# One product of a two-layer graph network as three one-pass matmuls instead of one fp32 matmul, with the work around it in another order

## The chip, the cores and the metric

The kernel runs on one core of a Trainium2 chip. The metric is device time in microseconds (us), the median of several executions. Engines: PE is TensorE (matmul), DVE is VectorE, ACT is ScalarE, POOL is GpSimd, SP is SyncE, which here only issues DMAs.

## The reference

For each of 8 graphs (C = 1024 nodes, D = 256 features, DH = 512 hidden), with H = (adj != 0), w the first row of adj, Dn = 1/(H w) and Be = 1/(column sums of H):

```
m  = Be * (H^T x)                      # S1
z  = H m                               # S2, kept transposed
h  = relu(Dn * (z W1^T) + b1)          # P
h  = layer_norm(h) * gamma + beta
q  = h W2^T                            # Q, gamma folded into W2, beta into a row
m2 = Be * (H^T q)                      # S3
x1 = layer_norm(x + Dn * (H m2) + b2 + x)      # S4
v  = x1 WL^T                           # V, both halves of WL
o  = relu(v_left + (adj v_right) / deg)        # L
out = layer_norm(x1 + o)
```

Input, output and weights are float32, x is [8, 1024, 256] and adj [8, 1024, 1024].

## The kernel before

The nodes lie in NT = 8 tiles of 128. Each engine has its instruction stream written out by hand, one body per graph, and the streams meet in semaphores; an engine takes its instructions strictly in the order written. PE runs the stages S1, S2, P/Q, S3, S4, V, L and then S1 of the next graph. A product that must be exact in fp32 is a plain F32 matmul; S1 to S4 have one factor of zeros and ones (H), so the other factor is split into a high and a low part of type F32R (a rounded fp32), and each part is one F32R matmul.

The stretch around the change is the loop over steps s, on PE as on DVE and ACT. S2 makes z^T in four PSUM banks: its first half (nodes 0 to 511) runs before the loop, eight k-steps of four matmuls with 512 columns; its second half is dealt out over the first four loop steps (`SECOND_CHUNK`, k-steps 3, 2, 2, 1). ACT copies z^T to `zT` (L480). Step s then holds on PE: P(s), two F32 matmuls of 512 columns (L893); from s = 3 the four transposes TH(s-3) of the hidden rows (L901); from s = 4 Q(s-4), four F32 matmuls of 256 columns (L909). On DVE: hrow = P(s) * rDn + b1 (L675), the inverse root and the centring of tile s-1 (L574, L579), `moments` of tile s (L583, L585), q_f32 = Q(s-4) + a row (L689). On ACT: relu (L487), xnT out of the transposes (L494), the square root for the variance (L440), x_hi, the high part of q (L501). POOL makes the low part (L388, semaphore `q_split`).

S3, S4 and L go through `tiled` (L777): a first pass over k with two output tiles at once (`GROUP`), each k waiting for its input (`ready`), then the remaining tiles one by one. In S3, ACT and DVE make m_hi (L435) and m_lo (L590) from each finished tile; `sum_Dn` of the next graph (L558) is queued on DVE behind m_lo of tiles 3 to 7, and waits for the load of `raw`, which SP issues once Q(7) is done:

```
sp.wait_ge(*full("Q", NT - 1, b))
load_graph(b + 1)
...
for e in range(NT):
    take_m_lo("S3", e, b, NT + e)
    if more and e >= DN_LAG:
        sum_Dn(e - DN_LAG, b + 1, (raw_loaded[(e - DN_LAG) // 2], (b + 1) * IN_B))
```

Before the first graph a prologue transposes adj on PE while S1 of graph 0 runs as rows of adj arrive: per row tile c, transposes, S1 for six output tiles, and one weight's transposes (`BETWEEN`). `sum_bW2` (L621) runs on DVE in c = 6, in front of the building of H for c = 7 (L543). `PRODUCT_BANKS` says which PSUM bank each output takes.

Of the kernel before, what the change touches and what calls it, by code (L numbers as in the profile page):

```python
# [5 lines left out]
F32 = mybir.dt.float32  # L6
# [21 lines left out]
}  # L28
TRANSPOSE_BANKS = (6, 7)
N_BANKS = 8  # L30
GROUP = 2
SECOND_CHUNK = {0: (0, 1, 2), 1: (3, 4), 2: (5, 6), 3: (7,)}
LAG_T = 3
LAG_Q = 4
H_SLOTS = 4
# [3 lines left out]
def graph_net(nc, x, adj, W1, b1, gamma, beta, W2, b2, WL, out):  # L39
# [21 lines left out]
    BETWEEN = {1: ("gamma",), 3: ("W1", "W1"), 5: ("WL", "WL"), 6: ("W2", "W2")}  # L61
# [3 lines left out]
    def add_set(name, part):  # L65
        n = len(set_of)
        set_of[name, part] = TRANSPOSE_BANKS[n % 2], n // 2
# [9 lines left out]
    setup_fills = [0] * N_SIDE + [(len(set_of) + 1) // 2, len(set_of) // 2]  # L77
# [22 lines left out]
    for s in range(NT + LAG_Q):  # L100
        if s < NT:
            add_job("P", s)
        if 0 <= s - LAG_T < NT:
            add_job("TH", s - LAG_T)
        if 0 <= s - LAG_Q < NT:
            add_job("Q", s - LAG_Q)
# [12 lines left out]
    with ctx:  # L119
# [21 lines left out]
        xres, _, _ = place("xres", [P, NT, D], F32)  # L141
        w_row, _, _ = place("w_row", [P, C], F32)
        W1T, _, _ = place("W1T", [P, ND, DH], F32)
# [5 lines left out]
        x1T, _, _ = place("x1T", [P, 2, ND, P], F32)  # L149
        q_f32, q_at, _ = place("q_f32", [P, 2, D], F32)  # L150
        o_f32, _, _ = place("o_f32", [P, 2, D], F32)
        ident, _, _ = place("ident", [P, P], F32)
        small, _, _ = place("small", [P, 20, NT], F32)

        zT, _, nxt = place("zT", [P, ND, C], F32, raw_at)
        hrow, _, nxt = place("hrow", [P, H_SLOTS, DH], F32, nxt)
        xnT, _, _ = place("xnT", [P, 2, NH, P], F32, nxt)
# [4 lines left out]
        yv, _, _ = place("yv", [P, NT, YP], F32, HT_at)  # L162

        unread, _, _ = place("unread", [P, C], F32, q_at)
# [6 lines left out]
        gamma_n, _, _ = place("gamma_n", [P, P], F32, nxt)  # L171

        def col(n):
# [3 lines left out]
         std_o, rstd_o, gb) = (col(n) for n in range(16))  # L177
        gamma_c, bW2_c, eps_c = gb[:, 0:NH], gb[:, NH:NH + ND], small[:, 16, 0:1]
        stats, _, _ = place("stats", [P, 3, NT, 6], F32)
# [27 lines left out]
        relu_done = sem("relu_done")  # L207
        deg_done, rdeg_done, o_done, sum_done = (sem(n) for n in ("deg_done", "rdeg_done", "o_done", "sum_done"))
# [60 lines left out]
        def _(sp):  # L269
# [44 lines left out]
            load_first_rows(6)  # L314
            load_first_rows(7)
# [39 lines left out]
        def _(pool):  # L355
# [13 lines left out]

            for j in range(NT // 2):  # L370
                pool.wait_ge(first_x_loaded[j], 16)
            pool.wait_ge(bias_loaded, 16 * 2)
            pool.wait_ge(rDn_ready, 1)
# [26 lines left out]
        def _(act):  # L400
# [61 lines left out]
            for c in range(NT):  # L462
                take_adjT(c, 0)
                if c in BETWEEN:
                    take_set(BETWEEN[c][0], 0)
                if c % 2 == 0 and c + 2 < NT:
                    split_first_x_hi(c // 2 + 1)
                take_adjT(c, 1)
                if len(BETWEEN.get(c, ())) > 1:
                    take_set(BETWEEN[c][1], 1)  # L470
            for e in range(NT):
                take_m_hi("S1", e, 0, e)

            def graph(b, more):
                def take_zT(ch):
                    for d in range(ND):
                        act.wait_ge(*full("S2", ch * ND + d, b))
                        act.wait_ge(HT_ready, b * NT + NT)
                        act.wait_ge(dn_ready, b * NT + NT)
                        empties_bank(nc.scalar.activation(zT[:, d, ch * CH:(ch + 1) * CH],  # L480
                                                          bank("S2", ch * ND + d)[:, :], ACT.Copy), "S2", ch * ND + d)

                take_zT(0)
                for s in range(NT + LAG_Q):
                    if s < NT:
                        act.wait_ge(*emptied("P", s, b))
                        nc.scalar.activation(hrow[:, s % H_SLOTS, :], hrow[:, s % H_SLOTS, :], ACT.Relu)\  # L487
                          .then_inc(relu_done, 1)
                    if s == max(SECOND_CHUNK) - 1:
                        take_zT(1)  # L490
                    if 0 <= s - LAG_T < NT:
                        i = s - LAG_T
                        act.wait_ge(*full("TH", i, b))
                        empties_bank(nc.scalar.activation(xnT[:, i % 2, :, :].rearrange("p k c -> p (k c)"),  # L494
                                                          bank("TH", i)[:, :], ACT.Copy), "TH", i)
                    if s < NT:
                        root("h", 0, std_h, s, b)
                    if s >= LAG_Q:
                        i = s - LAG_Q
                        act.wait_ge(*emptied("Q", i, b))  # L500
                        nc.scalar.activation(x_hi[:, i, 0:D], q_f32[:, i % 2, :], ACT.Copy).then_inc(q_hi_done, 1)  # L501
# [38 lines left out]
        def _(dve):  # L540
# [10 lines left out]
            def sum_Dn(c, b, loaded):  # L551
# [6 lines left out]
                nc.vector.scalar_tensor_tensor(out=unread[:, :], in0=raw[:, c, :], scalar=0.0, in1=w_row[:, :],  # L558
# [3 lines left out]
            def build_rDn(b):  # L562
# [4 lines left out]
                dve.wait_ge(rDn_part, b * 3 + 2)  # L567
                nc.vector.reciprocal(dn_inv, dn_safe).then_inc(rDn_part, 1)
                dve.wait_ge(rDn_part, b * 3 + 3)
                nc.vector.tensor_tensor(rDn, dn_inv, dn_pos, ALU.mult).then_inc(rDn_ready, 1)  # L570
# [11 lines left out]
            def moments(norm, which, src, i, b):  # L582
                nc.vector.bn_stats(stats[:, which, i, :], src)  # L583
                dve.drain()
                nc.vector.bn_aggr(mv[:, which, i, :], stats[:, which, i, :]).then_inc(var_done[norm], 1)  # L585
# [56 lines left out]
            for c in range(NT):  # L642
# [14 lines left out]
            for e in range(NT):  # L657
# [3 lines left out]
                if e == 0:  # L661
                    dve.wait_ge(*set_full("bW2", 0))
                    nc.vector.tensor_copy(bW2_row[:, :], set_bank("bW2", 0)[:, 0:D])\
                      .then_inc(bank_empty[set_of["bW2", 0][0]], 1)
                if N_SIDE - 3 <= e < N_SIDE:
                    sum_Dn(e + NT - N_SIDE, 0, (first_rows_loaded[e + NT - N_SIDE], 16))
            build_rDn(0)

            def graph(b, more):
                dve.wait_ge(bias_loaded, 16 * 2)  # L670
                dve.wait_ge(rDn_ready, b + 1)
                for s in range(NT + LAG_Q):
                    if s < NT:
                        dve.wait_ge(*full("P", s, b))
                        empties_bank(nc.vector.scalar_tensor_tensor(  # L675
                            out=hrow[:, s % H_SLOTS, :], in0=bank("P", s)[:, :], scalar=rDn[:, s:s + 1],
                            in1=b1_row[:, :], op0=ALU.mult, op1=ALU.add), "P", s)
                    if 0 <= s - 1 < NT:
                        inverse_root("h", std_h, rstd_h, s - 1, b)
                        centre("h", 0, hrow[:, (s - 1) % H_SLOTS, :], rstd_h, s - 1, b)  # L680
                    if s < NT:
                        dve.wait_ge(relu_done, b * NT + s + 1)
                        moments("h", 0, hrow[:, s % H_SLOTS, :], s, b)
                    if s >= LAG_Q:
                        i = s - LAG_Q
                        dve.wait_ge(*full("Q", i, b))
                        if i >= 2:
                            dve.wait_ge(q_split, b * NT + i - 1)
                        empties_bank(nc.vector.tensor_tensor(q_f32[:, i % 2, :], bank("Q", i)[:, 0:D],  # L689
                                                             bW2_row[:, :], ALU.add), "Q", i)  # L690
                if more:
                    dve.wait_ge(q_split, b * NT + NT)
                for e in range(NT):
                    take_m_lo("S3", e, b, NT + e)
                    if more and e >= DN_LAG:
                        sum_Dn(e - DN_LAG, b + 1, (raw_loaded[(e - DN_LAG) // 2], (b + 1) * IN_B))

                dve.wait_ge(xb_ready, b * NT + NT)
                for i in range(NT + 1):
# [14 lines left out]
                    if i < NT:  # L714
                        if i == 0:
                            dve.drain()
                        nc.vector.bn_aggr(mv[:, 1, i, :], stats[:, 1, i, :]).then_inc(var_done["1"], 1)

                nc.vector.memset(yv[:, :, 2 * D:YP], 1.0).then_inc(y_ones, 1)
                if more:  # L720
                    for c in range(NT):
                        build_H_tile(c, b + 1)
                        if c >= NT - DN_LAG:
                            sum_Dn(c, b + 1, (raw_loaded[c // 2], (b + 1) * IN_B))
# [39 lines left out]
        def _(pe):  # L764
# [12 lines left out]
            def tiled(stage, b, n_cols, ready, parts, operands, before_last=None):  # L777
# [10 lines left out]
                for k in range(NT):  # L788
                    ready(k)
                    for i in range(GROUP):  # L790
# [3 lines left out]
                for i in range(GROUP, NT):  # L794
# [46 lines left out]
            for c in range(NT):  # L841
                pe.wait_ge(first_rows_loaded[c], 16)
                transpose_adj(c, 0)
                pe.wait_ge(H_ready, c + 1)
                pe.wait_ge(x_split, c + 1)
                for e in range(N_SIDE):
# [4 lines left out]
                    if e == 3:  # L851
# [4 lines left out]
            transpose_set("bW2", 0)  # L856
# [118 lines left out]
```

## Time and profile before

| | us |
|---|---|
| runs, not profiled: median, lowest, highest of 3 | 1104.91, 1104.28, 1105.42 |
| the profiled execution's own time | 1105.18 |
| its span, first to last instruction | 1103.6 |
| PE busy | 1090.7 (99%) |
| DVE busy | 699.1 (63%) |
| ACT busy | 317.0 (29%) |
| POOL busy | 182.6 (17%) |

The span lies 1.58 us below the execution's own time. Matmuls overlap each other at their ends, so a busy PE is not yet one at full pace; the pace of a matmul is read from the distance between its neighbours. The granted TensorE clock was 0.999 of full over the run.

### The profile page before, as it was taken

The page shows a single profiled execution, that of the slowest core. Times are in us where ns is not written, and L with a number is a line of the kernel's source. Part 1 is how long each engine was busy: PE and PEld are TensorE (multiplying, and loading weights), DVE is VectorE, ACT ScalarE, POOL GpSimd, SP SyncE. Part 2 cuts the span into 40 slices and gives each one's busy share as a digit, 9 for nine tenths or more (in the row PEclk, how much of TensorE's full clock was granted, in tenths as well). Part 3 has the DMA queues.
Part 4 walks back from the last instruction along what each step waited for, and adds up shares of the span by engine and source line. Part 5 has one row for each costly group of instructions (what it writes and reads, how often), then busy time and mean ns, then how long its engine had stood idle before and what let it go on. Part 6 is the DMA issues. An engine that isn't in the chain of part 4 may idle for free.

```text
span 1103.6 us, 18550 instructions
## 1 busy us (share of the span) xinstructions
PE 1090.7 (99%) x6107; PEld 895.7 (81%) x6107; DVE 699.1 (63%) x1845; ACT 317.0 (29%) x710; POOL 182.6 (17%) x256
## 2 busy tenths in 40 slices
PE   7999999999999999999999999999999999999997
PEld 7779697796978979688796978969788696887966
DVE  5666595576854768548685486755776746856326
ACT  5342212422133321333113331233301433024230
POOL 0312013210122102111040120401104020041000
PEclk9999999999999999999999999999999999999999
DMA  8117611167212471134611445116433075300001
GB/s 291 39 21 153 153 59 38 25 127 152 57 38 51 102 160 48 38 80 102 132 48 38 105 106 112 48 28 134 105 84 74 2 152 115 66 10 1 1 1 39
DMA packets 63871, 86.44 MB, mean 78 GB/s; under 512 B 8164, under 2 KB 53864, under 8 KB 63848
## 3 DMA queue, kind: packets, MB, share of 16 engines
q1 hardware_dynamic: 63376, 85.75, 33.9%
q10 hardware_dynamic: 472, 0.40, 0.1%
q8 instruction: 13, 0.21, 0.1%
q14 instruction: 10, 0.08, 0.0%
HBM read 77.73 MB, written 8.39 MB: 78 GB/s over the span
## 4 chain that ended last, share of the span: by engine, by line
PE 93%; DVE 4%; DMA 1%; SPq 1%; ACT 1%; issue 0%; DVEq 0%; ACTq 0%
PE bank L783 40%; PE bank L871 10%; PE bank L909 10%; PE bank L931 10%; PE bank L893 10%; PE bank L811 9%; PE bank L901 3%; PE bank L917 1%; DMA raw<-in_adj_dram 1%; DVE adjT L603 1%; DVE HT L608 1%; DVE o_f L740 0%; DVE xres L744 0%; ACT m_hi L435 0%; DVE stats L583 0%
## 5 line engine op out<-in xcount | busy, mean ns | idle before, releaser
L783 PE MATMUL bank<-yv,adjT 128*128 128x257 f32 x1024 | 223.3, 379 | 0.0
L783 PEld LDWEIGHTS bank<-yv,adjT 128*128 128x128 f32 x1024 | 193.6, 189 | 31.8 <-issue 3.8
L440 ACT ACTIVATE small<-mv,small 128x1 f32<-128x1 f32 x192 | 56.6, 295 | 361.9 <-DVE mv L585 266.4
L811 PE MATMUL bank<-x_hi,H 128*128 128x258 f32 x512 | 124.6, 290 | 1.2 <-issue 0.6
L783 PE MATMUL bank<-x_hi,H 128*128 128x256 f32 x512 | 122.6, 283 | 0.0
L783 PE MATMUL bank<-m_hi,HT 128*128 128x256 f32 x512 | 121.5, 280 | 0.0
L783 PE MATMUL bank<-x_lo,H 128*128 128x256 f32 x512 | 121.1, 280 | 0.0
L783 PE MATMUL bank<-m_lo,HT 128*128 128x256 f32 x512 | 120.8, 279 | 0.0
L811 PE MATMUL bank<-x_lo,H 128*128 128x256 f32 x512 | 119.6, 282 | 0.9 <-DVE H L543 0.9
L893 PE MATMUL bank<-W1T,zT 128*128 128x512 f32 x256 | 120.3, 592 | 0.0
L590 DVE SCALAR_TENSOR_TENSOR m_lo<-bank,small,m_hi 128x256 fp32r<-128x256 f32 x128 | 61.0, 483 | 92.8 <-ACT m_hi L435 92.8
L909 PE MATMUL bank<-gW2T,xnT 128*128 128x256 f32 x512 | 119.8, 379 | 0.0
L931 PE MATMUL bank<-WLT,x1T 128*128 128x512 f32 x256 | 119.1, 593 | 0.0
L378 POOL TENSOR_TENSOR xres<-x_in 128x256 f32<-128x256 f32 x64 | 43.6, 716 | 451.9 <-DMA out_dram<-xres 411.5
L435 ACT ACTIVATE m_hi<-bank,small 128x256 fp32r<-128x256 f32 x128 | 59.9, 475 | 182.7 <-DVE small L635 94.8
L871 PE MATMUL bank<-HT,m_hi 128*128 128x512 f32 x256 | 110.4, 431 | 0.2 <-DVE m_lo L590 0.2
L675 DVE SCALAR_TENSOR_TENSOR hrow<-bank,small,b_row 128x512 f32<-128x512 f32 x64 | 47.8, 747 | 96.0 <-PE bank L893 96.0
L871 PE MATMUL bank<-HT,m_lo 128*128 128x512 f32 x256 | 101.7, 397 | 0.0
L909 PEld LDWEIGHTS bank<-gW2T,xnT 128*128 128x128 f32 x512 | 92.9, 190 | 10.3
L783 PEld LDWEIGHTS bank<-x_hi,H 128*128 128x128 f32 x512 | 96.8, 189 | 0.2
L783 PEld LDWEIGHTS bank<-x_lo,H 128*128 128x128 f32 x512 | 96.2, 188 | 0.2
L783 PEld LDWEIGHTS bank<-m_lo,HT 128*128 128x128 f32 x512 | 96.1, 188 | 0.0
(84 smaller groups left out, 1620.6 us busy)
## 6 DMA issues: line engine op xcount, KB each, us to landing
raw<-in_adj_dram SPq DMA_DIRECT2D x112, 256.0 KB, 8.6
adjB<-in_adj_dram SPq DMA_DIRECT2D x224, 128.0 KB, 3.4
x_in<-in_x_dram SPq DMA_DIRECT2D x31, 256.0 KB, 4.7
out_dram<-xres SPq DMA_DIRECT2D x108, 64.0 KB, 1.6
raw<-in_adj_dram SPq DMA_DIRECT2D x8, 512.0 KB, 10.3
w_row<-in_adj_dram SPq DMA_DIRECT2D x8, 512.0 KB, 3.6
out_dram<-xres SPq DMA_DIRECT2D x4, 256.0 KB, 2.2
W1n<-in_L_gnn_W_dram SPq DMA_DIRECT2D x1, 512.0 KB, 10.8
```

The source lines that it names most:

```text
L378: nc.gpsimd.tensor_tensor(xres[:, t, :], x_in[:, t, :], x_in[:, t, :], ALU.add).then_inc(xb_part, 1)
L435: nc.scalar.activation(m_hi[:, e, :], bank(stage, e)[:, 0:D], ACT.Identity, scale=rBe[:, e:e + 1])\
L440: nc.scalar.activation(std[:, i:i + 1], mv[:, which, i, 1:2], ACT.Sqrt, bias=eps_c)\
L590: empties_bank(nc.vector.scalar_tensor_tensor(out=m_lo[:, e, :], in0=bank(stage, e)[:, 0:D], scalar=rBe[:, e:e + 1], in1=m_hi[:, e, :].bit ...
L675: empties_bank(nc.vector.scalar_tensor_tensor(out=hrow[:, s % H_SLOTS, :], in0=bank("P", s)[:, :], scalar=rDn[:, s:s + 1], in1=b1_row[:, : ...
L783: last = mm(bank(stage, i)[:, 0:n_cols], lhsT, rhs, start=(k == 0 and part == 0), stop=(k == NT - 1 and part == parts - 1))
L811: last = mm(*args, start=(c == 0 and n == 0), stop=(c == NT - 1 and n == 1))
L871: last = mm(bank("S2", job)[:, :], m[:, k, d * P:(d + 1) * P], HT[:, k, ch * CH:(ch + 1) * CH], start=(k == 0 and n == 0), stop=(k == NT - ...
L893: last = mm(bank("P", s)[:, :], zT[:, d, s * P:(s + 1) * P], W1T[:, d, :], start=(d == 0), stop=(d == ND - 1))
L901: last = nc.tensor.transpose(bank("TH", i)[:, k * P:(k + 1) * P], hrow[:, i % H_SLOTS, k * P:(k + 1) * P], ident[:, :])
L909: last = mm(bank("Q", i)[:, 0:D], xnT[:, i % 2, k, :], gW2T[:, k, :], start=(k == 0), stop=(k == NH - 1))
L931: last = mm(bank("V", i)[:, :], x1T[:, i % 2, d, :], WLT[:, d, :], start=(d == 0), stop=(d == ND - 1))
```

## The change

P = z W1^T is no longer an F32 matmul. z and W1 are each split: high = F32R(value * ROUND_DOWN), low = value - high. W1_low is scaled by 4096 (SPLIT), W1_cross = W1_high - scaled W1_low, and z_cross = z_high * (1 + 1/4096) - z. P is put together from three F32R products, z_cross W1_cross in a PSUM bank of its own (stage "M"), and z_high W1_high + z_low W1_low in another. Per tile DVE adds the two with their scales: M first, hrow = M * rDn_cross + b1, and then hrow = P * rDn_main + hrow. Of z, ACT makes the high part (in place of the copy), DVE the low and the cross part, both read from PSUM. The centring of h goes from DVE to ACT (`centre_h`, with a shift that DVE computes). S2's second half is spread over steps 0 to 2 (k-steps 4, 2, 2). TH lags P by 2 and Q by 3 steps instead of 3 and 4; Q comes ahead of TH; S3's first pass takes four tiles and has Q(5) to Q(7) and TH(6), TH(7) between its first k-steps. The layout of banks and SBUF follows. In the prologue, rows 6 and 7 of adj are loaded ahead of W2 and beta, W2's transposes and `sum_bW2` move from c = 6 to c = 7, both transposes of row tile 0 come ahead of its H, bW2's transposes move into S1(6), and the splitting of W1 is added on ACT and POOL.

```diff
-SECOND_CHUNK = {0: (0, 1, 2), 1: (3, 4), 2: (5, 6), 3: (7,)}
-LAG_T = 3
-LAG_Q = 4
-H_SLOTS = 4
+SECOND_CHUNK = {0: (0, 1, 2, 3), 1: (4, 5), 2: (6, 7)}
+LAG_T = 2
+LAG_Q = 3
+H_SLOTS = 3
...
             load_first_rows(5)
             sp.dma_start(WLn[:, :, :], WL.rearrange("(t p) d -> p t d", p=P)).then_inc(WL_loaded, 16)
+            load_first_rows(6)
+            load_first_rows(7)
             sp.dma_start(W2n[:, :, :], W2.rearrange("(t p) d -> p t d", p=P)).then_inc(W2_loaded, 16)
...
# ACT
+                act.wait_ge(HT_ready, b * NT + NT)
+                act.wait_ge(dn_ready, b * NT + NT)
+                take_z_high(0, 0)
+                take_z_high(0, 1)
                 for s in range(NT + LAG_Q):
+                    if s == max(SECOND_CHUNK):
+                        take_z_high(1, 0)
+                    if 0 <= s - 1 < NT:
+                        root("h", 0, std_h, s - 1, b)
+                    if s == max(SECOND_CHUNK):
+                        take_z_high(1, 1)
+                    if s == 1:
+                        centre_h(0)
+                    if 0 <= s - LAG_T < NT:
+                        act.wait_ge(*full("TH", s - LAG_T, b))
+                        empties_bank(nc.scalar.activation(xnT[:, :, :].rearrange("p k c -> p (k c)"),
+                                                          bank("TH", s - LAG_T)[:, :], ACT.Copy), "TH", s - LAG_T)
                     if s < NT:
                         act.wait_ge(*emptied("P", s, b))
                         nc.scalar.activation(hrow[:, s % H_SLOTS, :], hrow[:, s % H_SLOTS, :], ACT.Relu)\
                           .then_inc(relu_done, 1)
+                    if 1 <= s - 1 < NT:
+                        centre_h(s - 1)
+                    if s > LAG_Q:
+                        take_x_hi(s - LAG_Q - 1)
+                take_x_hi(NT - 1)
...
# DVE
+                take_z_low(0, 0)
+                take_z_low(0, 1)
                 for s in range(NT + LAG_Q):
+                    if s in (1, 2):
+                        moments_h(s - 1)
+                    if s < NT:
+                        dve.wait_ge(*full("M", s, b))
+                        empties_bank(nc.vector.scalar_tensor_tensor(
+                            out=hrow[:, s % H_SLOTS, :], in0=bank("M", s)[:, :], scalar=rDn_cross[:, s:s + 1],
+                            in1=b1_row[:, :], op0=ALU.mult, op1=ALU.add), "M", s)
+                    if 2 < s <= NT:
+                        moments_h(s - 1)
+                    if s == 1:
+                        shift_of(0)
+                    if s == max(SECOND_CHUNK):
+                        take_z_low(1, 0)
                     if s < NT:
                         dve.wait_ge(*full("P", s, b))
+                        dve.wait_ge(*emptied("M", s, b))
                         empties_bank(nc.vector.scalar_tensor_tensor(
-                            out=hrow[:, s % H_SLOTS, :], in0=bank("P", s)[:, :], scalar=rDn[:, s:s + 1],
-                            in1=b1_row[:, :], op0=ALU.mult, op1=ALU.add), "P", s)
+                            out=hrow[:, s % H_SLOTS, :], in0=bank("P", s)[:, :], scalar=rDn_main[:, s:s + 1],
+                            in1=hrow[:, s % H_SLOTS, :], op0=ALU.mult, op1=ALU.add), "P", s)
+                    if 1 < s <= NT:
+                        shift_of(s - 1)
+                    if s == max(SECOND_CHUNK):
+                        take_z_low(1, 1)
+                    if s > LAG_Q:
+                        take_q(s - LAG_Q - 1)
+                take_q(NT - 1)
...
# PE
+                        for d in range(ND):
+                            last = mm(bank("M", s)[:, :], z_cross[:, d, nodes], W1_cross[:, d, :],
                                       start=(d == 0), stop=(d == ND - 1))
+                        fills_bank(last, "M", s)
+                        pe.wait_ge(*free("P", s, b))
+                        for d in range(ND):
+                            mm(bank("P", s)[:, :], z_high[:, d, nodes], W1_high[:, d, :], start=(d == 0), stop=False)
+                            last = mm(bank("P", s)[:, :], z_low[:, d, nodes], W1_low[:, d, :],
+                                      start=False, stop=(d == ND - 1))
                         fills_bank(last, "P", s)
+                    if s >= LAG_Q:
+                        take_product_Q(s - LAG_Q)
+                    if s >= LAG_T:
+                        transpose_hidden(s - LAG_T)
...
                 tiled("S3", b, D, lambda c: pe.wait_ge(q_split, b * NT + c + 1), 2,
-                      lambda c, e, part: (H_columns(c, e), (x_hi, x_lo)[part][:, c, 0:D]))
+                      lambda c, e, part: (H_columns(c, e), (x_hi, x_lo)[part][:, c, 0:D]),
+                      group=4, behind_k=last_of_Q)
```

`take_z_low(ch, d)` is one subtraction (z_low, PSUM minus SBUF) and one scalar_tensor_tensor (z_cross, SBUF and PSUM), 512 columns each; `moments_h` is L583 and L585; `shift_of` is the reciprocal L574 and a 128x1 tensor_scalar; `take_q` is L689; `last_of_Q(c)` is Q(5+c) and TH(6+c), as far as there are any.

## Rows read from the trace of the kernel before

**Rows 1.** The page's first part: busy time and share of the span.

```profile
PE 1090.7 (99%) x6107; PEld 895.7 (81%) x6107; DVE 699.1 (63%) x1845; ACT 317.0 (29%) x710; POOL 182.6 (17%) x256
```

**Rows 2.** The critical chain in one graph: start us, us, what.

```profile
439.99 10.27 PE bank L871 x44
...
451.97 1.86 PE bank L871 x8
...
469.97 1.72 PE bank L893 x4
471.69 0.44 PE bank L901 x4
472.13 1.73 PE bank L909 x8
...
485.96 28.28 PE bank L783 x240
```

**Rows 3.** Groups of instructions by line and form, whole span.

```profile
L590 DVE SCALAR_TENSOR_TENSOR m_lo<-bank,small,m_hi 128x256 fp32r<-128x256 f32 x128 | 61.0, 483 | 92.8 <-ACT m_hi L435 92.8
L435 ACT ACTIVATE m_hi<-bank,small 128x256 fp32r<-128x256 f32 x128 | 59.9, 475 | 182.7 <-DVE small L635 94.8 <-PE bank L783 87.9
L675 DVE SCALAR_TENSOR_TENSOR hrow<-bank,small,b_row 128x512 f32<-128x512 f32 x64 | 47.8, 747 | 96.0 <-PE bank L893 96.0
L740 DVE SCALAR_TENSOR_TENSOR o_f<-bank,small,yv 128x256 f32<-128x256 f32 x64 | 30.6, 478 | 0.3
L689 DVE TENSOR_TENSOR q_f<-bank,bW_row 128x256 f32<-128x256 f32 x64 | 26.9, 420 | 44.9 <-PE bank L909 44.9
```

**Rows 4.** Timeline of VectorE in one loop step: start us, us, what [idle before].

```profile
471.73 0.75 DVE L675 SCALAR_TENSOR_TENSOR hrow<-bank,small,b_row 128x512 f32<-128x512 f32 x1 [1.12 <-PE bank L893]
472.39 0.15 DVE L574 RECIPROCAL small<-small 128x1 f32<-128x1 f32 x1
472.59 0.55 DVE L579 TENSOR_SCALAR hrow<-hrow,mv,small 128x512 f32<-128x512 f32 x1
473.18 0.69 DVE L583 BATCH_NORM_STATS2 stats<-hrow 128x6 f32<-128x512 f32 x1
473.95 0.18 DVE L585 BATCH_NORM_AGGREGATE mv<-stats 128x2 f32<-128x6 f32 x1
474.13 0.43 DVE L689 TENSOR_TENSOR q_f<-bank,bW_row 128x256 f32<-128x256 f32 x1
```

**Rows 5.** Timeline of ScalarE in the same graph's loop.

```profile
447.15 1.09 ACT L480 ACTIVATE zT<-bank 128x512 f32<-128x512 f32 x2 [1.85 <-PE bank L871]
...
476.40 0.63 ACT L487 ACTIVATE hrow<-hrow 128x512 f32<-128x512 f32 x1 [1.39 <-DVE hrow L675]
476.93 0.58 ACT L494 ACTIVATE xnT<-bank 128x512 f32<-128x512 f32 x1
478.04 0.29 ACT L440 ACTIVATE small<-mv,small 128x1 f32<-128x1 f32 x1 [0.53 <-DVE mv L585]
478.38 0.42 ACT L501 ACTIVATE x_hi<-q_f 128x256 fp32r<-128x256 f32 x1
478.71 0.58 ACT L494 ACTIVATE xnT<-bank 128x512 f32<-128x512 f32 x1
```

**Rows 6.** Timeline of SyncE in the same graph: issue of the load of raw.

```profile
485.99 7.82 SPq L273 DMA_DIRECT2D raw<-in_adj_dram  x16
```

**Rows 7.** Timeline of VectorE in S3 of the same graph: `sum_Dn` of tiles 2 and 4.

```profile
498.23 1.22 DVE L558 SCALAR_TENSOR_TENSOR unread<-raw,w_row 128x1024 f32<-128x1024 f32 x1
...
502.46 1.23 DVE L558 SCALAR_TENSOR_TENSOR unread<-raw,w_row 128x1024 f32<-128x1024 f32 x1 [0.38 <-DMA raw<-in_adj_dram]
```

**Rows 8.** Timeline of TensorE in the prologue.

```profile
23.54 0.66 PE L774 MATMUL bank<-ident,raw 128*128 128x128 f32 x4 [0.37 <-DMA raw<-in_adj_dram]
24.69 0.36 PE L811 MATMUL bank<-x_hi,H 128*128 128x258 f32 x1 [0.49 <-DVE x_lo L639]
...
29.13 0.38 PE L811 MATMUL bank<-x_lo,H 128*128 128x256 f32 x1 [0.89 <-DVE H L543]
```

More of the change, by code:

```diff
@@ L65, in add_set @@
     def add_set(name, part):
-        n = len(set_of)
-        set_of[name, part] = TRANSPOSE_BANKS[n % 2], n // 2
+        tb = TRANSPOSE_BANKS[0 if name == "bW2" else len(set_of) % 2]
+        set_of[name, part] = tb, sum(other == tb for other, _ in set_of.values())
     for c in range(NT):
@@ L76, in graph_net @@
     add_set("bW2", 0)
-    setup_fills = [0] * N_SIDE + [(len(set_of) + 1) // 2, len(set_of) // 2]
+    setup_fills = [0] * N_SIDE + [sum(other == tb for other, _ in set_of.values()) for tb in TRANSPOSE_BANKS]
     setup_empties = [1] * N_SIDE + setup_fills[N_SIDE:]
@@ L171, in graph_net @@
         gamma_n, _, _ = place("gamma_n", [P, P], F32, nxt)
+        W1T, _, _ = place("W1T", [P, ND, DH], F32, xres_at)
         def col(n):
@@ L176, in graph_net @@
         (dn, dn_pos, dn_safe, dn_inv, rDn, be_safe, rBe, deg_safe, rdeg, std_h, rstd_h, std_1, rstd_1,
-         std_o, rstd_o, gb) = (col(n) for n in range(16))
+         std_o, rstd_o, gb, rDn_main, rDn_cross, shift_h) = (col(n) for n in (*range(16), 18, 19, 20))
         gamma_c, bW2_c, eps_c = gb[:, 0:NH], gb[:, NH:NH + ND], small[:, 16, 0:1]
-        stats, _, _ = place("stats", [P, 3, NT, 6], F32)
+        stats, _, _ = place("stats", [P, NT, 6], F32)
         mv, _, _ = place("mv", [P, 3, NT, 2], F32)
@@ L470, in _ @@
                     take_set(BETWEEN[c][1], 1)
+                if c == 4:
+                    for d in range(ND):
+                        act.wait_ge(*set_empty("W1", d))
+                        nc.scalar.activation(W1_high[:, d, :], W1T[:, d, :], ACT.Copy, scale=ROUND_DOWN)\
+                          .then_inc(W1_high_done, 1)
+                if c == NT - 2:
+                    for d in range(ND):
+                        act.wait_ge(W1_low_done, d + 1)
+                        nc.scalar.activation(W1_low[:, d, :], W1_low[:, d, :].bitcast(F32), ACT.Copy, scale=SPLIT)\
+                          .then_inc(W1_low_scaled, 1)
@@ L471, in _ @@
             for e in range(NT):
                 take_m_hi("S1", e, 0, e)
+                if e == 0:
+                    act.wait_ge(*set_full("bW2", 0))
+                    nc.scalar.activation(bW2_row[:, :], set_bank("bW2", 0)[:, 0:D], ACT.Copy)\
+                      .then_inc(bank_empty[set_of["bW2", 0][0]], 1)
             def graph(b, more):
[L475 to L481, printed above, removed]
@@ L549, in build_H_tile, with sum_Dn @@
                                         ALU.not_equal).then_inc(H_ready, 1)
-            def sum_Dn(c, b, loaded):
+            def sum_Dn(c, b, into, loaded):
                 dve.wait_ge(*loaded)
@@ L557, in sum_Dn @@
                     dve.wait_ge(dn_ready, b * NT + c)
-                nc.vector.scalar_tensor_tensor(out=unread[:, :], in0=raw[:, c, :], scalar=0.0, in1=w_row[:, :],
+                nc.vector.scalar_tensor_tensor(out=into[:, :], in0=raw[:, c, :], scalar=0.0, in1=w_row[:, :],
                                                op0=ALU.not_equal, op1=ALU.mult,
@@ L670, in graph, with take_z_low @@
                 dve.wait_ge(bias_loaded, 16 * 2)
-                dve.wait_ge(rDn_ready, b + 1)
-                for s in range(NT + LAG_Q):
+                dve.wait_ge(rDn_ready, b * 2 + 2)
+                def take_z_low(ch, d):
+                    cols = slice(ch * CH, (ch + 1) * CH)
+                    dve.wait_ge(z_high_done, b * (NCH * ND) + ch * ND + d + 1)
+                    nc.vector.tensor_tensor(z_low[:, d, cols], bank("S2", ch * ND + d)[:, :],
+                                            z_high[:, d, cols].bitcast(F32), ALU.subtract).then_inc(z_low_done, 1)
+                    empties_bank(nc.vector.scalar_tensor_tensor(
+                        out=z_cross[:, d, cols], in0=z_high[:, d, cols].bitcast(F32), scalar=1.0 + 1.0 / SPLIT,
+                        in1=bank("S2", ch * ND + d)[:, :], op0=ALU.mult, op1=ALU.subtract), "S2", ch * ND + d)
@@ new lines, in take_q, with moments_h @@
+                def take_q(i):
+                    dve.wait_ge(*full("Q", i, b))
+                    if i >= 2:
+                        dve.wait_ge(q_split, b * NT + i - 1)
+                    empties_bank(nc.vector.tensor_tensor(q_f32[:, i % 2, :], bank("Q", i)[:, 0:D],
+                                                         bW2_row[:, :], ALU.add), "Q", i)
+                take_z_low(0, 0)
+                take_z_low(0, 1)
+                def moments_h(i):
+                    dve.wait_ge(relu_done, b * NT + i + 1)
+                    moments("h", 0, hrow[:, i % H_SLOTS, :], i, b)
@@ L775, in transpose_four, with tiled @@
                 last.then_inc(bank_full[tb], 1)
-            def tiled(stage, b, n_cols, ready, parts, operands, before_last=None):
+            def tiled(stage, b, n_cols, ready, parts, operands, group=2, behind_k=None, before_last=None):
                 def one(i, k):
@@ L789, in tiled @@
                     ready(k)
-                    for i in range(GROUP):
+                    for i in range(group):
                         if k == 0:
@@ L793, in tiled @@
                         one(i, k)
-                for i in range(GROUP, NT):
+                    if behind_k:
+                        behind_k(k)
+                for i in range(group, NT):
                     if i == NT - 1 and before_last:
@@ L850, in _ @@
                         transpose_set(BETWEEN[c][0], 0)
-                    if e == 3:
+                    if e == 3 and c > 0:
                         transpose_adj(c, 1)
@@ L859, in _ @@
                 for c in range(NT):
+                    if e == N_SIDE and c == NT // 2:
+                        transpose_set("bW2", 0)
                     s1_step(e, c, 0)
@@ L883, in graph, with take_product_Q, transpose_hidden, last_of_Q @@
                 pe.wait_ge(HT_ready, b * NT + NT)
-                for s in range(NT + LAG_Q):
+                def take_product_Q(i):
+                    pe.wait_ge(*free("Q", i, b))
+                    pe.wait_ge(*emptied("TH", i, b))
+                    for k in range(NH):
+                        last = mm(bank("Q", i)[:, 0:D], xnT[:, k, :], gW2T[:, k, :],
+                                  start=(k == 0), stop=(k == NH - 1))
+                    fills_bank(last, "Q", i)
+                def transpose_hidden(i):
+                    pe.wait_ge(*free("TH", i, b))
+                    pe.wait_ge(normed["h"], b * NT + i + 1)
+                    for k in range(NH):
+                        last = nc.tensor.transpose(bank("TH", i)[:, k * P:(k + 1) * P],
+                                                   hrow[:, i % H_SLOTS, k * P:(k + 1) * P], ident[:, :])
+                    fills_bank(last, "TH", i)
+                def last_of_Q(c):
+                    i = NT - LAG_Q + c
+                    if i < NT:
+                        take_product_Q(i)
+                    if i + 1 < NT:
+                        transpose_hidden(i + 1)
+                for s in range(NT):
                     for k in SECOND_CHUNK.get(s, ()):
@@ L904, in graph @@
-                    i = s - LAG_Q
-                    if 0 <= i < NT:
-                        pe.wait_ge(*free("Q", i, b))
-                        pe.wait_ge(*emptied("TH", i, b))
-                        for k in range(NH):
-                            last = mm(bank("Q", i)[:, 0:D], xnT[:, i % 2, k, :], gW2T[:, k, :],
-                                      start=(k == 0), stop=(k == NH - 1))
-                        fills_bank(last, "Q", i)
+                        fills_bank(last, "M", s)
```

148 lines of the change are left out of this document (77 added, 71 removed), and 15 rows, old and new, of the table PRODUCT_BANKS.

## The prediction

> **What bounds the kernel now.** First the page's busy shares: PE 99%, DVE 63%, ACT 29% [rows 1]. Busy alone doesn't say that PE is the bound, since matmul records overlap, so next the critical chain of one graph [rows 2]. In this graph every piece is a PE piece and each begins where the last ended; its times are ends of work, so a piece divided by its count is the pace. F32R, 512 columns (S2): 10.27 / 44 = 0.233 us. Fp32, 512 columns (P): 1.72 / 4 = 0.43 us for a record, and a matmul of P has two records, so 0.86. F32R, 256 columns (S3): 28.28 / 240 = 0.118. Four transposes: 0.44. A Q of four matmuls: 1.73. So PE is the bound inside a graph, and PE time removed is time gained as long as no other engine is late. The last view is thus the timelines of DVE and ACT in the loop [rows 4, 5]: I read from them both durations and the distance from one start to the next, which is shorter (0.66 for a scalar_tensor_tensor of 512 columns that lasts 0.75; the next starts while the last one drains).
>
> **What PE is rid of.** A tile of P costs 1.72 now (two fp32 matmuls, four records). After: two F32R matmuls for M and four for P, all with 512 columns and new stationary columns each time, just as in S2: 6 x 0.233 = 1.40. The difference, 0.32, times 64 tiles is 20.5 us. S2's second half, the transposes, Q and S3 keep their number of matmuls and only change place: no PE cost. The bound on the other side: at the 0.215 of an fp32 pass (0.43 for two) [rows 2] the tile would cost 1.29, and the saving is 27.5. I take 0.233, since S2 has the same type, size and change of weights; nothing excludes the other fully.
> [...]
>
> **What the other engines get, steady steps.** I lay out a step that begins on PE at T. PE: M ends at T+0.47, P at T+1.40, Q(s-3) at T+3.13, TH(s-2) at T+3.57; so a step takes 3.57. A reader starts 0.04 behind the end of a matmul group or of another engine's operation (P ends at 471.69, DVE starts at 471.73) [rows 2, 4].
> DVE per step: two scalar_tensor_tensor (2 x 0.67), moments (0.76 to the second operation's start, 0.18 more to its end [rows 4]), reciprocal and shift (0.30), q (0.42): about 3.0 of 3.57, so it fits. The new forms are priced by neighbours: z_low as L689 (0.420 at 256 columns) plus the 0.27 that 256 more columns add between L740 and L675, so 0.69 long and 0.62 from start to start; z_cross as L675, 0.747 and 0.67. Writing fp32r instead of fp32 costs nothing (L590 483 ns, L740 478 ns) [rows 3].
> ACT per step: root 0.34, xnT 0.53, relu 0.53, centring as relu with per-row operands (0.55 to 0.7; L435 against L501 at 256 columns is 0.06 more), x_hi 0.33: 2.3 of 3.57 [rows 3, 5]. Its order matters: relu(s) stands behind xnT(s-2), which waits for PE's last work of the step. xnT from T+3.61, relu(s) done at about T+4.7, and DVE wants it behind M of step s+1, at T+4.9. xnT(s-2) is done at T+4.2 and PE wants it for Q at T+4.97. Both just fit, so a steady step stays at PE's 3.57. The removed centring on DVE (0.59) pays for most of the second addition.
>
> **Step 0.** t = 0 is the end of S2's first half (439.99 + 32 x 0.233 = 447.46) [rows 2]. ACT starts z_high at t = -0.31 and has both by 0.8 [rows 5]; DVE runs four operations, 2 x (0.62 + 0.67), from 0.32 to 3.0. PE has 16 matmuls of S2, 3.73, as cover. No stall; without the cover it would be 3 us.
>
> **Steps 2 to 4, where it breaks.** PE's ends without stalls: M(2) 10.74, P(2) 11.67, TH(0) 12.11, M(3) 12.58, P(3) 13.51, Q(0) 15.24, TH(1) 15.68, M(4) 16.15, P(4) 17.08. DVE starts M(2) at 10.84 (behind moments(1), which waits for relu(1)). From there it has no idle time: M(2) 0.67, z_low 0.62, z_cross 0.67, P(2) 0.67, shift 0.30, z_low 0.62, z_cross 0.67 (all z read at 15.1; PE wants that at 15.5, so M(4) just passes), M(3) 0.67, moments(2) 0.94: variance at 16.67. On ACT root(2) stands ahead of xnT(1): 16.71, xnT(1) 17.05 to 17.63. Q(1) could have been issued at 16.9 and is issued at 17.67: a stall of 0.75. By step 5 DVE has caught up (its 3.0 in 3.57). The stall pushes all of PE, so 8 graphs x 0.75 = 6.0 us lost. Bounds: 0 (if DVE's operations overlap by 0.1 more each) and 1.5 (if each is 0.1 longer).
>
> **Q within S3.** The first pass has 8 x 8 x 0.118, and between its k-steps Q(5), TH(6), Q(6), TH(7), Q(7). From S3's start: xnT(5) 0.7, wanted 0.94; xnT(6) 3.8, wanted 4.05; xnT(7) 6.9, wanted 7.2; the high part of q(7) 9.9, which leaves POOL 2.7 us for the low part. No stall, with 0.25 to spare at three places; lateness of 0.3 in one costs 0.1 to 0.3 per graph, and I put that into the range.
>
> **Load of raw.** SP issues it behind Q(7): before at 485.99, 15.1 before S3's end (128 x 0.118). Q(7) now ends 8.9 into S3, whose own length with the Qs is 21.15, so only 12.2 before the end. DVE's m_lo(6), m_lo(7) are queued behind `sum_Dn` of tiles 2 and 3, which need the second pair of raw tiles. It had landed by 12.2 (498.23, no wait) [rows 6, 7]; the third came at 16.45, the whole load of four pairs is issued over 7.8, so about 11.6 for the second. Then m_lo(7) is ready 3.1 behind S3's end and S4 wants it after 3.3: nothing to nothing, at worst (12.2) 0.4 x 7 = 2.8 us. `sum_Dn` of tile 4 ends 2 us late and S4's evacuation on DVE begins late by that; it runs at 1.4 per tile against PE's 1.9 and catches up.
>
> **Prologue.** PE waits in it at c = 6 (0.37 for the row, 0.49 for x_lo) and at c = 7 (0.89 for H, which stood behind `sum_bW2`) [rows 8], with weight transposes of 0.44 each on the path after them. Rows 6 and 7 now come ahead of 0.75 MB, and H(7) ahead of `sum_bW2`; m_lo moves forward by 2 us too. I take 2.5 of gain; bounds 1 and 3.4. The splitting of W1 on ACT and POOL lies in their gaps and is needed only at P(0), 15 us later.
>
> **Sum.** 1105.2 (the profiled execution's own time) - 20.5 + 6.0 - 2.5 = 1088.2. The runs' median is 0.3 below that execution: **1087.9 us**.
>
> **Rivals.**
> A, the faster pace: F32R at 0.215. For it: the fp32 row. Against: every S2 piece. Gain 7.0 more, of which the stall takes back 0.35 x 8, since DVE's chain doesn't shorten: about 1084. [...] Chance 0.08.
> B, the stall is absent or under 0.3, as DVE overlaps more than I add up: 1082 to 1085. Chance 0.12.
> C, DVE or ACT lag for more steps, 1.5 to 2 us per graph, as three margins are only 0.1 to 0.25: 1092 to 1100. For it: DVE's load in steps 2 to 4 has no gap. Against: 0.5 us regained in each later step. Chance 0.17.
> D, slower: the load of raw holds DVE in S3, so m_lo(7) and S4 are late in 7 graphs. Each us past the margin costs 7; it decides from 2.8 us late (17.3 + 2.2 of gain and bound, by 7), that is a second pair that lands after 15. Against: 12.2 is the row. With it, that F32R products run as two passes (6 x 0.43, 1160 us), which S2 speaks against. Chance 0.05 together; 0.03 for no change, gain eaten by a mixture.
> The forecast, 1085 to 1092: 0.55.
>
> Within 0.2% (2.2 us) a measurement of this kernel can't tell a change from none. Faster: 0.55 + 0.08 + 0.12 + 0.17 = 0.92; same 0.03, slower 0.05. The range leaves out D, no change and the far end of C: 1082 to 1097.
>
> **What would show it.** The chain: F32R pieces of P and M at 0.233, 1.40 per tile; steps of 3.57 from s = 5 on. PE or its chain shows one break of 0.5 to 1 us per graph, at Q(1), released by ACT xnT, behind DVE's moments(2). M(0) and M(4) don't wait. Each graph gets about 1.8 us shorter. S2 of the first graph starts 2 to 3 us earlier. I am wrong if DVE idles in steps 2 to 4, if S4 waits for m_lo, or if PE waits for xnT in every step.

## The result and the profile after

The changed kernel takes 1093.44 us (4 runs, 1093.02 to 1093.75) against 1104.74; the ratio is 0.9893, 95% interval 0.9881 to 0.9905. That is faster by 11.3 us, inside the range of 1082 to 1097, and 5.5 us above the forecast of 1087.9. The profiled execution took 1093.02, its span is 1091.4.

The critical chain of the graph that [rows 2] show, now (start us, us, what):

```profile
436.95 11.20 PE bank L967 x48
448.15 0.46 PE bank L1017 x2
...
449.31 0.24 PE bank L1023
449.56 0.03 issue
...
460.93 0.04 ACT small L466
460.97 0.16 issue
461.13 0.58 ACT xnT L546
461.72 0.04 issue
461.76 1.99 PE bank L985 x8
463.75 0.44 PE bank L993 x4
464.19 0.46 PE bank L1017 x2
464.65 0.24 PE bank L1022
464.89 0.23 PE bank L1023
...
465.58 1.73 PE bank L985 x8
467.31 0.44 PE bank L993 x4
...
483.90 25.48 PE bank L874 x216
...
569.70 0.47 PE bank L967 x2
```

From this S2 to the next, 436.95 to 569.70, is 132.75 us; before it was 134.57 (439.99 to 574.56 in the same view). So a graph got 1.82 shorter; forecast 1.8. A tile of P costs 0.46 + 4 x 0.23 = 1.4. From the transposes behind Q(1) on, a step takes 3.55 or 3.56 (463.75 to 467.31 is the first). The chain leaves PE behind P(0), at 449.56, runs through DVE and ACT, and comes back to PE at Q(1); the timeline of ScalarE says why:

```profile
460.93 0.29 ACT L466 ACTIVATE small<-mv,small 128x1 f32<-128x1 f32 x1 [1.69 <-DVE mv L643]
461.13 0.58 ACT L546 ACTIVATE xnT<-bank 128x512 f32<-128x512 f32 x1
```

ACT idles 1.69 in front of the root (L466), for moments(2), and xnT(1) stands behind it. PE pays for it in each graph, as the waits show (us in total, times, longest; PEld is TensorE loading the stationary operand):

```profile
PEld bank L985 <- ACT xnT L546: 5.4, 7, 0.8
PE bank L985 <- ACT xnT L546: 2.8, 8, 0.4
```

The loop came out as forecast. But eight graphs of 1.82 are 14.6 us, and only 12.2 of span are gone. The rest is in the prologue. S2 of graph 0 ends its first half (start of its 32nd matmul) at 45.40, before at 42.83: 2.6 later, where 2.5 earlier was forecast. The longest waits of PE between 0 and 60 us, apart from that for the first row of adj (4.4; before 4.6 for two rows):

```profile
PE bank L865 <- DVE bW_wide L684: 1.4, 1, 1.4
PE bank L904 <- DVE x_lo L697: 1.4, 1, 1.4
PE bank L967 <- DVE m_lo L648: 1.0, 1, 1.0
```

All three are for DVE; the fourth, 0.3, is for ACT. The timeline of VectorE there:

```profile
18.06 1.22 DVE L613 SCALAR_TENSOR_TENSOR unread<-raw,w_row 128x1024 bf16<-128x1024 f32 x1
...
20.41 2.31 DVE L613 SCALAR_TENSOR_TENSOR unread<-raw,w_row 128x1024 bf16<-128x1024 f32 x1
...
22.65 1.75 DVE L598 TENSOR_SCALAR H<-raw 128x1024 fp32r<-128x1024 f32 x1
...
27.95 2.29 DVE L613 SCALAR_TENSOR_TENSOR unread<-raw,w_row 128x1024 bf16<-128x1024 f32 x1
...
30.38 1.56 DVE L679 SCALAR_TENSOR_TENSOR unread<-W2n,beta_row 128x512 bf16<-128x512 f32 x1
...
38.76 0.47 DVE L648 SCALAR_TENSOR_TENSOR m_lo<-bank,small,m_hi 128x256 fp32r<-128x256 f32 x1
...
39.42 1.53 DVE L613 SCALAR_TENSOR_TENSOR unread<-raw,w_row 128x1024 bf16<-128x1024 f32 x1
```

and that of GpSimd:

```profile
20.21 3.63 POOL L389 TENSOR_TENSOR W_low<-W1T,W_high 128x512 fp32r<-128x512 f32 x2 [18.73 <-ACT W_high L500]
27.49 3.89 POOL L393 TENSOR_TENSOR W_cross<-W_high,W_low 128x512 fp32r<-128x512 f32 x2 [3.65 <-ACT W_low L505]
34.86 6.57 POOL L404 TENSOR_TENSOR xres<-x_in 128x256 f32<-128x256 f32 x8 [3.47 <-DVE HT L655]
```

The same instruction of the same shape takes 1.22 us and then 2.31. Those that got longer are those that began while GpSimd worked: four beside W_low and W_cross by 1.09, 1.06, 1.07 and 0.87, the three sums beside the residual by 0.3 to 0.4. Behind the sums, three of DVE's six short operations on 8 columns lose another 0.2 to 0.5 each beside it. The sums write bf16 now where they wrote fp32, but that is not what lengthens them: alone they take 1.22 in both kernels. The residual used to start at 41.9, behind this stretch; the change lets it start at HT, by an edit that the description of the change does not name:

```diff
-            pool.wait_ge(rDn_ready, 1)
+            pool.wait_ge(W1_low_done, ND)
+            pool.wait_ge(HT_ready, NT)
```

m_lo, which reads PSUM and one tensor in SBUF, keeps its 0.47 even beside the residual.

### The profile page after: what moved, and what is told of

Same layout as the page of the kernel before. It is cut to its first block, busy times and chain, and to the rows that moved or that the text cites. A ratio compares the mean times of both kernels' runs of the same rounds, so it can differ in the third digit from the quotient of the medians.

```text
span 1091.4 us, 18826 instructions
## 1 busy us (share of the span) xinstructions
PE 1073.9 (98%) x6235; PEld 919.8 (84%) x6235; DVE 755.0 (69%) x1988; ACT 356.9 (33%) x779; POOL 196.8 (18%) x260
## 4 chain that ended last, share of the span: by engine, by line
PE 83%; DVE 11%; ACT 2%; issue 2%; DMA 1%; DVEq 1%; SPq 0%
PE bank L874 40%; PE bank L1050 10%; PE bank L985 9%; PE bank L904 8%; PE bank L967 7%; PE bank L993 2%; DVE stats L641 2%; DVE hrow L760 1%; PE bank L1023 1%; PE bank L1022 1%; PE bank L1017 1%; PE bank L1035 1%; DMA raw<-in_adj_dram 1%; DVE hrow L772 1%; ACT hrow L550 1%
## 5 line engine op out<-in xcount | busy, mean ns | idle before, releaser
L466 ACT ACTIVATE small<-mv,small 128x1 f32<-128x1 f32 x192 | 56.6, 295 | 357.1 <-DVE mv L643 258.7
L985 PE MATMUL bank<-gW2T,xnT 128*128 128x256 f32 x512 | 123.1, 383 | 2.8 <-ACT xnT L546 2.8
L874 PE MATMUL bank<-x_hi,H 128*128 128x256 f32 x512 | 125.7, 287 | 0.0
L967 PE MATMUL bank<-HT,m_hi 128*128 128x512 f32 x256 | 101.1, 395 | 1.1 <-DVE m_lo L648 1.0
L414 POOL TENSOR_TENSOR x_lo<-q_f,x_hi 128x256 fp32r<-128x256 f32 x64 | 43.3, 682 | 295.3 <-ACT x_hi L529 295.3
L874 PEld LDWEIGHTS bank<-m_hi,HT 128*128 128x128 f32 x512 | 96.1, 188 | 0.0
```

What stands on the lines that cost most here:

```text
L414: nc.gpsimd.tensor_tensor(x_lo[:, i, :], q_f32[:, i % 2, :], x_hi[:, i, 0:D].bitcast(F32), ALU.subtract).then_inc(q_split, 1)
L466: nc.scalar.activation(std[:, i:i + 1], mv[:, which, i, 1:2], ACT.Sqrt, bias=eps_c)\
L874: last = mm(bank(stage, i)[:, 0:n_cols], lhsT, rhs, start=(k == 0 and part == 0), stop=(k == NT - 1 and part == parts - 1))
L967: last = mm(bank("S2", job)[:, :], m[:, k, d * P:(d + 1) * P], HT[:, k, ch * CH:(ch + 1) * CH], start=(k == 0 and n == 0), stop=(k == NT - ...
L985: last = mm(bank("Q", i)[:, 0:D], xnT[:, k, :], gW2T[:, k, :], start=(k == 0), stop=(k == NH - 1))
```

## Experiments

Theory G: GpSimd's instructions hold VectorE's, and PE waits for that. Theory O: the new order of loads, `sum_bW2` and transposes costs the time. Theory Q, for the loop: Q(1) waits because xnT(1) is queued behind root(2). The kernel before, timed again beside these runs, took 1104.97 (the first four), 1104.46 (the old orders, W1 on VectorE, W1 in pieces) and 1104.95 (the last two), so a difference of less than 0.5 between runs of different groups says nothing by itself.

**The residual late.**

```diff
-            pool.wait_ge(HT_ready, NT)
+            pool.wait_ge(rDn_ready, 2)
```

> The changed kernel with one line back: GpSimd's residual of graph 0 waits again for rDn instead of for HT, so it runs behind VectorE's prologue work. Theory G (GpSimd work holds VectorE instructions that read two tensors in SBUF or run in a faster mode): the three sums of Dn in S1/S2 fall from about 1.6 to 1.22 us, TensorE's wait of 1.4 us for m_lo in S2 of graph 0 goes, 1.1 us gained: 1092.3 us. Theory O (the order of loads, of sum_bW2 and of the bW2 transposes is what costs): those sums stay as they are, 1093.4 us.

Measured: 1092.34 us, ratio 0.9886 (0.9871 to 0.9901). The three sums are back at 1.23, 1.22 and 1.23. As theory G has it.

**W1's split for 8 of 512 columns.** W1_cross likewise; the rest of both is zero, so P lacks those parts of W1.

```diff
-                nc.gpsimd.tensor_tensor(W1_low[:, d, :], W1T[:, d, :], W1_high[:, d, :].bitcast(F32), ALU.subtract)\
+                nc.gpsimd.tensor_tensor(W1_low[:, d, 0:8], W1T[:, d, 0:8], W1_high[:, d, 0:8].bitcast(F32), ALU.subtract)\
...
```

> The changed kernel, where GpSimd computes W1_low and W1_cross for 8 of 512 columns only (the rest is zero, so P lacks those parts): four short GpSimd operations in place of 7.5 us of them. Theory G: the VectorE operations at 20.4, 22.7, 28.0 and 30.4 us fall from 2.31, 1.75, 2.29 and 1.56 us to 1.22, 0.69, 1.22 and 0.69; TensorE's waits for x_lo and bW2 shrink by about 3.5 us: 1090 us. Theory O: within 0.5 us of 1093.4.

Measured: 1089.40 us, ratio 0.9859 (0.9843 to 0.9874). The order is that of the changed kernel, but the operations are short again (VectorE's timeline of this run):

```profile
20.78 1.23 DVE L615 SCALAR_TENSOR_TENSOR unread<-raw,w_row 128x1024 bf16<-128x1024 f32 x1
...
21.94 0.68 DVE L600 TENSOR_SCALAR H<-raw 128x1024 fp32r<-128x1024 f32 x1
```

It regained 4.0 us, a little more than the 3.5 expected, nearly all of the 4.1 that the four operations had lost.

**Both.** 

> Both edits together, the residual late and W1's split for 8 columns. Theory G: the sum of the two, 4.6 us, 1088.8 us, that is, the prologue gains the 2.5 us that was forecast. Theory O: 1093 us.

Measured: 1088.22 us, ratio 0.9847 (0.9833 to 0.9860): 5.2 us regained, which is within 0.3 of the 1087.9 forecast for the change. The first half of S2 in graph 0 ends at 40.54, 2.3 earlier than before the change.

**xnT(1) ahead of root(2).**

```diff
-                    if 0 <= s - 1 < NT:
+                    if 0 <= s - 1 < NT and s != 3:
                         root("h", 0, std_h, s - 1, b)
...
+                    if s == 3:
+                        root("h", 0, std_h, s - 1, b)
                     if s < NT:
                         act.wait_ge(*emptied("P", s, b))
```

> The changed kernel with one exchange on ScalarE: in step 3 xnT(1) comes ahead of root(2). Theory Q (the break in the loop is xnT(1) queued behind root(2), which waits for moments(2)): the wait at Q(1) goes in all 8 graphs, 0.5 us each: 1089.4 us. Rival: VectorE is behind anyway, and the wait moves to the next step's xnT or M: 1092 to 1093.4 us, with a new wait at Q(2) or TH(2).

Measured: 1089.66 us, ratio 0.9861 (0.9846 to 0.9876): 3.8 us, 0.47 per graph. PE's waits for xnT are gone, and what is left in their place, before the transposes TH, is small:

```profile
PEld bank L995 <- ACT hrow L523: 1.7, 7, 0.2
```

Counted from the start of S2, the transposes behind Q(1) begin at 26.19 in this run (435.84 to 462.03 in its chain) and at 26.80 in the changed kernel (436.95 to 463.75), so the break at Q(1) was 0.61. In this run those transposes and the next Q take 0.51 and 1.83 in place of 0.44 and 1.73: 0.17 of the 0.61 comes back there, a small part of what the rival expected, and the rest is gained. The chain around it:

```profile
435.84 11.20 PE bank L969 x48
...
460.30 1.73 PE bank L987 x8
462.03 0.51 PE bank L995 x4
...
463.92 1.83 PE bank L987 x8
```

**The old order, GpSimd's work left in.** Loads of rows 6 and 7 again behind W2 and beta, W2's transposes and `sum_bW2` again in c = 6, bW2's transposes again ahead of S1(6), banks to match. 

> The changed kernel with the prologue's order of before (rows 6 and 7 of adj behind W2 and beta, W2's transposes and sum_bW2 in c = 6, both banks' order, bW2's transposes ahead of S1(6)), GpSimd's added work left in. What is the new order worth when GpSimd disturbs it? Theory G: the first pair of GpSimd operations now falls into VectorE's wait for row 6, the second pair still costs about 2 us; the order's own gain of 2.5 us is missing: 1094 to 1095 us. Theory O (the new order costs): 1091 us or less.

Measured: 1094.31 us, ratio 0.9904 (0.9890 to 0.9918), inside theory G's range and against theory O, which had 1091 or less. Of the first pair of GpSimd's operations H(6) loses 0.2 and x_lo 1.1 (1.84 for its two operations in place of 0.75), of the second pair a sum and an HT lose 1.1 each (VectorE's timeline of this run):

```profile
23.25 1.84 DVE L697 TENSOR_TENSOR x_lo<-x_in,x_hi 128x256 fp32r<-128x256 f32 x2
...
32.04 1.77 DVE L655 TENSOR_SCALAR HT<-adjT 128x1024 fp32r<-128x1024 f32 x1
```

**The old order, GpSimd free.** The same with the residual late and W1's split for 8 columns. 

> Old prologue order, residual late, and W1's split for 8 of 512 columns (P lacks the rest of W1_low and W1_cross): the prologue of before with the new loop. Against the same kernel in the new order (1088.2 us) it shows what the order alone is worth: forecast in the prediction 2.5 us, so 1090.7 us, and against the kernel before it is the loop alone: 8 x 1.8 = 14.6 us less than 1104.9, 1090.3 us. Theory O: 1088 or less.

Measured: 1090.41 us, ratio 0.9869 (0.9854 to 0.9885). Without the residual's early start and most of the split, the kernel in the old order is 3.9 us faster than with them (1094.31): they cost in both orders. Against the same kernel in the new order (1088.22) the new order gains 2.2 us by the medians, and 2.7 when each is compared with the kernel before timed beside it; theory O had a loss. The two traces show only 1.2 (S2's first half in graph 0 ends at 41.74 here), but in this one some rows of adj came earlier (H of row tile 3 begins at 12.78, there at 13.78). So the sign is shown, and the size is somewhere between 1.2 and 2.7. Against the kernel before, the gain is nearly the loop's alone: 14.05 us.

**W1's subtractions on VectorE.** A whole kernel, with the residual late and xnT(1) first; GpSimd's two loops over W1 are gone, ACT's scaling of W1_low comes behind its m_hi, and on DVE:

```diff
+            for d in range(ND):
+                dve.wait_ge(W1_high_done, d + 1)
+                nc.vector.tensor_tensor(W1_low[:, d, :], W1T[:, d, :], W1_high[:, d, :].bitcast(F32), ALU.subtract)\
+                  .then_inc(W1_low_done, 1)
             build_rDn(0)
+            for d in range(ND):
+                dve.wait_ge(W1_low_scaled, d + 1)
+                nc.vector.tensor_tensor(W1_cross[:, d, :], ...).then_inc(W1_cross_done, 1)
```

> A whole kernel: the changed one with the residual late, xnT(1) ahead of root(2), and W1's four subtractions on VectorE behind the last m_lo of graph 0, in place of GpSimd. Theory G: it gains 4.6 + 3.8 us, and pays once: VectorE starts z_low later by 4 x 0.61 us, of which 0.5 to 1 is covered, so M(0) of graph 0 waits about 1.5 us: 1086.5 us. If the 2.5 us are covered by VectorE's idle time ahead of z_low (1.1 us in the run with the residual late, more with W1 gone from GpSimd): 1084.5 us.

Measured: 1085.38 us, ratio 0.9824 (0.9810 to 0.9838), between the two figures. W1_cross, which meets the residual, takes 1.70 for its two operations; W1_low, which meets nothing, 1.28. M(0) waited (PE's waits):

```profile
PE bank L1018 <- DVE z_cross L733: 0.7, 1, 0.7
```

**W1's subtractions in pieces of 128 columns.** Also a whole kernel, GpSimd as before, each of the four operations in four. 

> A whole kernel: the changed one with the residual late, xnT(1) ahead of root(2), and each of GpSimd's four W1 subtractions cut into four of 128 columns. If a GpSimd instruction holds VectorE for as long as it lasts, a colliding VectorE operation now loses at most some 0.4 us in place of 1.07: three quarters of 3.5 us come back, 1092.3 - 3.8 - 2.2 = 1086 to 1087 us. If what counts is GpSimd's total time, VectorE loses as much as before: 1088.5 us.

Measured: 1087.71 us, ratio 0.9845 (0.9831 to 0.9859), between the two. An operation of VectorE that meets a piece now loses about 0.25, not 1.07, but more of them meet one:

```profile
21.62 0.94 DVE L604 TENSOR_SCALAR H<-raw 128x1024 fp32r<-128x1024 f32 x1
22.48 1.28 DVE L703 TENSOR_TENSOR x_lo<-x_in,x_hi 128x256 fp32r<-128x256 f32 x2
...
24.56 1.47 DVE L619 SCALAR_TENSOR_TENSOR unread<-raw,w_row 128x1024 bf16<-128x1024 f32 x1
```

Added up over the stretch it is 3.2 us in place of 4.1; 0.5 of it is the copy for bW2:

```profile
30.82 0.89 DVE L690 COPY bW_wide<-small 128x128 f32<-128x128 f32 x2
```

It takes 0.36 in the changed kernel, where nothing runs beside it. GpSimd's own 7.5 us became 13.8 (7.62 and 6.17 for the two halves), so ACT's scaling of W1_low came later and PE waited 0.9 for adjT behind it.

**Free, and xnT(1) first.** 

> New prologue order, residual late, W1's split for 8 of 512 columns (P lacks the rest of W1_low and W1_cross), xnT(1) ahead of root(2): the changed kernel without any hold by GpSimd and without the wait at Q(1). If the two effects are independent they add: 1088.2 - 3.8 = 1084.4 us. If the wait at Q(1) partly hid something in the prologue or the other way round: 1085.5 or more.

Measured: 1084.36 us, ratio 0.9811 (0.9797 to 0.9824). The effects add.

**The residual behind W1_cross.** The kernel with W1 on VectorE and one more wait of GpSimd, for W1_cross_done. 

> The kernel with W1's subtractions on VectorE, and GpSimd's residual of graph 0 behind the last of them, so that it no longer meets W1_cross (1.70 us for the two there, 1.28 for W1_low's two, which met nothing). Theory G: 0.4 us less wait at M(0) of graph 0 (0.7 to 0.9 there): 1085.0 us. If that wait has another cause: 1085.4 us, unchanged.

Measured: 1084.92 us, ratio 0.9816 (0.9802 to 0.9829). W1_cross takes 1.29 for the two, M(0) waits 0.3, 0.4 less, as theory G has it (VectorE's timeline, then PE's waits):

```profile
38.88 1.29 DVE L717 TENSOR_TENSOR W_low<-W1T,W_high 128x512 fp32r<-128x512 f32 x2
...
40.94 1.29 DVE L722 TENSOR_TENSOR W_cross<-W_high,W_low 128x512 fp32r<-128x512 f32 x2
```

```profile
PE bank L1019 <- DVE z_cross L734: 0.3, 1, 0.3
```

The times alone would not show that 0.4: single executions of this kernel (1084.56 to 1085.32) and of the one with W1 on VectorE (1084.94 to 1085.50) overlap. This kernel has the lowest median of those that leave nothing out, 8.5 us below the change as given, and 0.6 above the one with most of W1's split left out: the split costs little in that place.

## Why the prediction was right, and where its size was off

**PE's saving.** Right: F32R products of P at 0.23, 1.40 a tile, as S2 paced them [rows 2]. Rival A's 0.215 is refuted by the pieces of P themselves.

**The steady steps.** Right: 3.55 or 3.56 against 3.57, DVE about 3.0 busy. The centring on ACT lasts 0.80, and what follows it starts 0.70 behind it, the upper end of the 0.55 to 0.7 allowed; ACT had room for it. PE waited for M(0) or M(4) in no graph, as forecast.

**The stall in steps 2 to 4.** Right in place and cause, shown by the exchange of two instructions. Forecast 0.75; the break measured 0.61, of which the exchange regains 0.47 (the mean of eight graphs). The issue of Q(1) was forecast for t = 17.67 from the end of S2's first half, and came at 17.3 (461.76 - 444.42). Two sizes were off: z_low and z_cross start 0.60 apart, not 0.62 and 0.67, and xnT(1) starts 0.20 behind root(2), not 0.34. Against the 0.14 that the smaller break gives stand small delays of Q within S3, for which nothing was in the sum: Q(5) to Q(7) take 1.80, 1.75 and 1.81 in the chain instead of 1.73, 0.17 together. So the graph's 1.82 met the forecast of 1.8 partly by luck: two small errors cancelled.

**The load of raw.** Right: the second pair came 11.5 after the first issue (forecast 11.6; DVE waited 1.6 for it), and PE waited for no m_lo in S3 or S4. Rival D did not occur.

**The prologue.** This is the term that was mis-sized: "I take 2.5 of gain" measured 2.6 of loss. The step that failed is its last sentence, "The splitting of W1 on ACT and POOL lies in their gaps". They were GpSimd's gaps, but not VectorE's: beside GpSimd's 7.5 us of splitting, VectorE lost 4.1. Left out altogether was the moved wait of the residual, which alone cost 1.1; the splitting cost 4.0. With GpSimd out of the way S2's first half in graph 0 ends at 40.54 instead of 42.83, 2.3 earlier, close to the 2.5; how much of that the order gives is shown to 1.2 to 2.7 only. The two sizes, 2.5 and 2.6, make 5.1 of the 5.5 us of error. The measured size lies outside the bounds for this term, 1 and 3.4 of gain. The trace of before had it already, in S1 of the graph of [rows 2], and so had its groups by form. A mean of 0.776, where a single operation takes 0.68, was the place to look. VectorE's rows, then the group:

```profile
432.47 0.68 DVE L608 TENSOR_SCALAR HT<-adjT 128x1024 fp32r<-128x1024 f32 x1
...
436.33 0.96 DVE L608 TENSOR_SCALAR HT<-adjT 128x1024 fp32r<-128x1024 f32 x1
```

```profile
L608 DVE TENSOR_SCALAR HT<-adjT 128x1024 fp32r<-128x1024 f32 x56 | 42.8, 776 | 0.0
```

GpSimd's, beside them:

```profile
433.39 5.51 POOL L378 TENSOR_TENSOR xres<-x_in 128x256 f32<-128x256 f32 x8 [59.07 <-DMA out_dram<-xres]
```

**The mechanism.** Shown: which VectorE operations lengthen beside GpSimd (two tensors in SBUF: the sums, x_lo, W1_cross; one tensor in SBUF: H and HT by tensor_scalar, the copy for bW2), which don't (m_lo beside the residual, with one tensor in PSUM and one in SBUF), that the loss vanishes with GpSimd's work, and that it falls to 0.25 when the pieces are a quarter. The page "SBUF — State Buffer" of the Trainium skill, section "Who interferes with whom", says that VectorE and GpSimd share a pair of ports as an exclusive lock; that a VectorE instruction with two SBUF inputs contends there with a GpSimd instruction that reads SBUF; and that one in a two-port mode and GpSimd block each other, whoever issues first having the pair for the whole instruction. The traces agree: up to 1.09 lost per hit beside 512 columns, 0.25 beside 128. That the lock is the cause, and not another shared resource with the same pattern, is the page's word; no run here shows the ports, or the mode in which H, HT and the copy ran.

## What to carry to other kernels

Work put on an idle GpSimd isn't free if VectorE is dense there: look for VectorE operations of one shape with two durations, and ask which engine ran beside the longer ones. When a wait is moved, price what now runs at the same time, and not just what is queued behind it. A queue order can be checked step by step on paper: a stall of 0.61 us per graph was found so, and one exchange regained 0.47 of it.

## What was not expected of the hardware

Cutting GpSimd's operations into quarters shortened each hold (0.25 instead of 1.07), but GpSimd's own time for the same columns rose from 7.5 to 13.8 us. Beside VectorE, GpSimd is slowed as well: the residual's first eight operations took 6.57 us beside the sums, and 4.62 in the run with the residual late, with VectorE on z, whose operations read one tensor from PSUM. The numbers fit two engines that take turns: against GpSimd's 16 pieces VectorE ran 14 operations of the kinds that collide, and a piece took 0.86 on average, about as long as one of those. That is a reading of the rows; no run tests it.
